# A four-layer graph network on one core: the third layer sums over the edges before its weight product

## What is computed

```python
x = x + L0(h)   # x1 = h @ W1 + b1 (512 wide), four gated sums over the edges, concatenated
x = x + L1(h)   # h @ W.T + bias, W scattered from edge_weight
x = x + L2(h)   # GCN, the layer of the change
x = x + L3(h)   # attention over the edges, elu
```

```python
deg = segment_sum(1, dst + loops); dinv = rsqrt(deg)
h = h @ W
out = segment_sum(h[src] * (dinv[src] * dinv[dst])[:, None], dst) + b
return relu(out)
```

## Time and profile before

| | us |
|---|---|
| three runs | 1003.13, 1002.95, 1000.69; median 1002.95 |
| the profiled execution | 1001.58, span 1000.0 |
| PE busy | 977.4 |
| DVE, ACT, POOL busy | 668.7, 430.9, 140.4 |

### The profile page before, as it was taken

How to read it: one execution, slowest core, us unless ns; L and a number is a source line. 1 busy time by engine, 2 the same in 40 slices (tenths; PEclk the granted TensorE clock), 3 DMA queues, 4 the chain that set the end, 5 groups by cost and what they waited for, 6 DMA issues and landing times.

```text
span 1000.0 us, 14720 instructions
## 1 busy us (share of the span) xinstructions
PE 977.4 (98%) x5170; PEld 809.6 (81%) x5170; DVE 668.7 (67%) x1221; ACT 430.9 (43%) x650; POOL 140.4 (14%) x191
## 2 busy tenths in 40 slices
PE   5999999999999999999999999999999999999997
PEld 3788788888888888888888888888888888888886
DVE  7877888788778879354485343216446664988886
ACT  5688865554543646112242322233222232445543
POOL 3022500000000010232221000000110000333331
PEclk9999999999999999999999999999999999999999
DMA  7256580000000014745433111243451230101223
GB/s 251 101 177 222 136 255 1 1 22 0 0 21 0 0 12 104 178 171 188 180 124 116 42 42 43 77 155 106 156 180 69 69 121 0 43 22 64 84 84 122
DMA packets 27326, 93.42 MB, mean 93 GB/s; under 512 B 3530, under 2 KB 3530, under 8 KB 27136
## 3 DMA queue, kind: packets, MB, share of 16 engines
q1 hardware_dynamic: 16400, 58.07, 16.5%
q0 software_dynamic: 10880, 34.74, 11.4%
HBM read 64.48 MB, written 33.56 MB: 98 GB/s over the span
## 4 chain that ended last, share of the span: by engine, by line
PE 91%; DVE 5%; ACT 2%; issue 1%; POOL 1%; DMA 0%; ACTq 0%; DVEq 0%; POOLq 0%
PE ps L592 32%; PE ps L2052 11%; PE ps L1972 9%; PE ps L1974 9%; PE ps L1973 9%; PE ps L2025 5%; PE ps L2024 5%; PE ps L575 3%; PE ps L1895 1%; PE ps L1897 1%; PE ps L1896 1%; PE ps L1866 1%; PE ps L1822 1%; PE ps L1825 1%; PE ps L1838 1%
## 5 line engine op out<-in xcount | busy, mean ns | idle before, releaser
L1972 PE MATMUL ps<-g_hi,mask_hi 128*128 128x512 f32 x400 | 157.4, 394 | 2.1 <-DVE mask_lo L1513 2.1
L1974 PE MATMUL ps<-g_hi,mask_lo 128*128 128x512 f32 x400 | 155.9, 390 | 0.0
L1973 PE MATMUL ps<-g_lo,mask_hi 128*128 128x512 f32 x400 | 155.7, 389 | 0.0
L558 ACT ACTIVATE hT_hi<-ps 128x1024 fp32r<-128x1024 f32 x40 | 41.0, 1025 | 200.3 <-PE ps L575 200.3
L592 PE MATMUL ps<-w_hi,hT_hi 128*128 128x512 f32 x320 | 126.4, 395 | 0.0
L592 PE MATMUL ps<-w_lo,hT_hi 128*128 128x512 f32 x320 | 124.7, 390 | 0.0
L2052 PE MATMUL ps<-y_all,att_hi 128*128 128x512 f32 x400 | 110.0, 393 | 1.5 <-DVE att_lo L1693 1.5
L1110 ACT ACTIVATE mask<-ps,v 128x640 f32<-128x640 f32 x80 | 63.4, 793 | 111.2 <-PE ps L1974 52.9
L592 PE MATMUL ps<-w_hi,hT_lo 128*128 128x512 f32 x320 | 98.6, 389 | 0.0
L1972 PEld LDWEIGHTS ps<-g_hi,mask_hi 128*128 128x128 f32 x400 | 75.1, 188 | 20.4 <-DVE mask_lo L1513 3.3
L2052 PEld LDWEIGHTS ps<-y_all,att_hi 128*128 128x128 f32 x400 | 74.0, 188 | 17.3 <-DVE att_lo L1693 1.5
(11 more groups left out here) (203 smaller groups left out, 1839.2 us busy)
## 6 DMA issues: line engine op xcount, KB each, us to landing
xin<-x_after SPq DMA_DIRECT2D x30, 512.0 KB, 3.3
xres<-x_after POOLq DMA_DIRECT2D x20, 512.0 KB, 4.2
x_after<-xres POOLq DMA_DIRECT2D x20, 512.0 KB, 3.0
w_raw<-in_L_gnn_W SPq DMA_DIRECT2D x8, 1024.0 KB, 7.2
x_after<-g POOLq DMA_DIRECT2D x20, 256.0 KB, 7.4
xres<-x_after SPq DMA_DIRECT2D x10, 512.0 KB, 3.4
xin<-in_x SPq DMA_DIRECT2D x9, 512.0 KB, 3.4
out_x<-xres SPq DMA_DIRECT2D x9, 512.0 KB, 2.7
```

Source lines behind the costliest of these rows:

```text
L1972: nc.tensor.matmul(SUMS[dd], mask_hi[k][:, cols], g_hi[:, s, :], start=(s == 0), stop=False)
L1973: nc.tensor.matmul(SUMS[dd], mask_hi[k][:, cols], g_lo[:, s, :], start=False, stop=False)
L1974: last = nc.tensor.matmul(SUMS[dd], mask_lo[k][:, cols], g_hi[:, s, :], start=False, stop=(s == T - 1))
```

## The change

The third layer is computed as (C h) W. Its parts:

- **Rows.** There is no reload of `x` for the third layer's norm. While the second layer's product runs, DVE takes the statistics of the finished rows in `xres` (`hs_stats_of`), ACT subtracts the mean and applies relu (`hs_relu`) and makes the high part times scale and dinv (`hs_hi_of`), DVE the low part (`hs_lo_of`). POOL's reload of `xres` waits for that relu. The loops over the second layer's tiles are written out.
- **Sums.** Six passes: two halves f of the 1024 features, by three ranges c of destination nodes of 512, 226 and 512 columns (in the order 0, 2, 1). A pass has ten steps; a step holds blocks of normed rows stationary (four blocks of features, high and low) and moves the counts of the range, converted by ACT into a ring of four. The result is already transposed for the product; it leaves PSUM as a high part (ACT) and a low part (DVE) into `sums_w` and `sums_x`, a pair of banks at a time. Passes alternate between two sets of four banks.
- **Product.** `gcn_product`, 48 matmuls of 512 columns per tile, the transposed sums stationary, W moving; then `gcn_out` as before, now per tile.
- **Weights.** W of the third layer is loaded after the third pass and split in the fifth and sixth; W of the last layer is loaded after the last pass and split beside the products, its destination taking the place of sums that are used up.
- The five semaphores `mask_used` and `cnt_used` become one each; nothing else of the first layer is changed.

```diff
+WIDTHS = (BANK, BANK, N - 2 * BANK)
+PASSES = [(f, c) for f in range(2) for c in (0, 2, 1)]
+COUNT_RING = 4
@@ DVE
+        def hs_stats_of(t):
+            b = t % 2
+            dve.wait_ge(res_added, t + 1)
+            for half in range(2):
+                hs_step_done(nc.vector.bn_stats(stats[b][:, half, :], xres[b][:, half * 512:(half + 1) * 512]))
...
+        def hs_scale_of(i):
+            dve.wait_ge(hs_root_ready, i + 1)
+            hs_step_done(nc.vector.reciprocal(rough[:, :], hs_root[:, :]))
+            dve.wait_ge(hs_chain, hs_steps[0])
+            hs_step_done(nc.vector.tensor_tensor(square[:, :], rough[:, :], rough[:, :], ALU.mult))
...
+        def hs_lo_of(t):
+            dve.wait_ge(hs_hi_ready, t + 1)
+            dve.wait_ge(hs_scale_ready, t // 2 + 1)
+            nc.vector.scalar_tensor_tensor(hs[:, :, t, 1, :], hs_f[:, :, t, 1, :], hs_scale[:, t % 2:t % 2 + 1], hs[:, :, t, 0, :].bitcast(F32),
+                                           ALU.mult, ALU.subtract).then_inc(hs_lo_ready, 1)
...
-        dense_dve(dve, d2, y_rest, late=self_loops)
+        for t in range(T):
+            if t >= 3:
+                hs_lo_of(t - 3)
+            if t + 2 < T:
+                stats_dve(dve, d1, (t + 2) // 2, t % 2)
+            if t + 1 < T:
+                transposed_dve(dve, d1, (t + 1) // 2, (t + 1) % 2)
+            if t % 2 == 1 and t + 2 < T:
+                variance_dve(dve, d1, (t + 2) // 2)
+            if t >= 1:
+                hs_stats_of(t - 1)
+            if t % 2 == 0 and t >= 2:
+                hs_variance_of(t // 2 - 1)
+            if t == 2:
+                self_loops()
+            residual(t)
+            if t % 2 == 1 and t + 2 < T:
+                scale_dve(dve, d1, (t + 2) // 2)
+            if t % 2 == 0 and t >= 2:
+                hs_scale_of(t // 2 - 1)
@@ ACT
+        for t in range(T):
+            if t % 2 == 1 and t >= 3:
+                hs_hi_of(t - 3)
+            if t + 1 < T:
+                transposed_act(act, d, (t + 1) // 2, (t + 1) % 2)
+            if t + 2 < T:
+                h_act(act, d, (t + 2) // 2, t % 2)
+            if t % 2 == 1 and t >= 3:
+                hs_hi_of(t - 2)
+            if t == T - 1:
+                for n in range(COUNT_RING):
+                    counts_act(n)
+            if t >= 1:
+                hs_relu(t - 1)
...
+        for n in range(T * len(PASSES)):
+            if n + COUNT_RING < T * len(PASSES):
+                counts_act(n + COUNT_RING)
+            if n == 0:
+                hs_relu(T - 1)
+            if n == 1:
+                hs_root_of(HT - 1)
+            if n == 2:
+                hs_hi_of(T - 2)
+            if n == 3:
+                hs_hi_of(T - 1)
+            if n == last_pass - HT:
+                split_act(act, dense[2], range(2))
+            if last_pass <= n < last_pass + KT - 2:
+                act.wait_ge(cnt_used, n + 1)
+                split_act(act, dense[2], [n - last_pass + 2])
+            if n % T >= T - 2:
+                sums_hi_of(n // T, n % T - (T - 2))
@@ PE
-        dense_pe(pe, dense[1], dense[2], lambda b: pe.wait_ge(sum_read, T * GATES - HT + 2 + b))
-        dense_pe(pe, dense[2])
+        dense_pe(pe, dense[1], lambda b: pe.wait_ge(sum_read, T * GATES - HT + 2 + b))
+        def gcn_pass(p):
+            f, c = PASSES[p]
+            sums = [PASS_BANKS[p % 2][j // 2][:, j % 2 * BANK:j % 2 * BANK + WIDTHS[c]] for j in range(4)]
+            for s in range(T):
+                n = T * p + s
+                if p == 0:
+                    pe.wait_ge(hs_lo_ready, s + 1)
+                pe.wait_ge(cnt_ready, n + 1)
+                columns = cnt[n % COUNT_RING][:, 0:WIDTHS[c]]
...
+                    for j in (2 * pair, 2 * pair + 1):
+                        nc.tensor.matmul(sums[j], hs[:, f, s, 0, j * P:(j + 1) * P], columns, start=(s == 0), stop=False)
...
+                    for j in (2 * pair, 2 * pair + 1):
+                        last = nc.tensor.matmul(sums[j], hs[:, f, s, 1, j * P:(j + 1) * P], columns, start=False, stop=(s == T - 1))
...
+        def gcn_product(t):
+            b = t % 2
+            pe.wait_ge(product_read[b], dense[2].pairs(t // 2))
+            pe.wait_ge(sums_lo_ready, 2 * PASSES.index((1, t // PASS_TILES)) + 2)
...
+                for part, rights in ((0, (W_HI[2], W_LO[2])), (1, (W_HI[2],))):
+                    for half in range(2):
+                        for right in rights:
+                            last = nc.tensor.matmul(PRODUCT[2][b][:, half * BANK:(half + 1) * BANK], sums_tile(t, part)[:, k, :],
+                                                    right[k][:, half * BANK:(half + 1) * BANK],
```

More of the change, by code:

```diff
@@ L306, in build_program, with __init__, norm_pairs @@
     class Dense:
-        def __init__(self, n):
+        def __init__(self, n, norm):
             self.n = n
+            self.norm = norm
         def pairs(self, i):
             return HT * self.n + i
+        def norm_pairs(self, i):
+            return HT * self.norm + i
         def tiles(self, t):
[L316 to L324, removed]
+            return T * self.norm + t
+    dense = [Dense(0, 0), Dense(1, 1), Dense(2, None), Dense(3, 2)]
     dst_landed = sem("dst_landed")
@@ L519, in scale_dve @@
         settled(dve, norm_chain0, done + 4)
[L520 to L526, removed]
+        nc.vector.tensor_tensor(scale[:, :], rough[:, :], step[:, :], ALU.mult).then_inc(scale_ready, 1)
     def scale_pool(pool, i):
@@ L651, in dense_act, with sums_place, sums_bank, sums_tile @@
         transposed_act(act, d, HT - 1, 1)
[L652 to L657, removed]
-        finish(HT - 1, 0)
[L659 to L664, removed]
-        finish(HT - 1, 1)
-        if nxt is not None:
-            root_act(act, nxt, 0)
+        finish(HT - 1, 0)
+        late()
+        finish(HT - 1, 1)
+    def sums_place(p, pair, part):
+        f, c = PASSES[p]
+        blocks = slice(4 * f + 2 * pair, 4 * f + 2 * pair + 2)
+        if c < 2:
+            return sums_w[:, PASS_TILES * c:PASS_TILES * (c + 1), part, blocks, :]
+        return sums_x[:, :, part, blocks, :]
+    def sums_bank(p, pair):
+        f, c = PASSES[p]
+        tiles = PASS_TILES if c < 2 else T - 2 * PASS_TILES
+        return PASS_BANKS[p % 2][pair].rearrange("p (k n) -> p k n", n=BANK)[:, :, 0:tiles * P].rearrange("p k (t n) -> p t k n", n=P)
+    def sums_tile(t, part):
+        return sums_w[:, t, part, :, :] if t < 2 * PASS_TILES else sums_x[:, t - 2 * PASS_TILES, part, :, :]
     def load_weights(eng, d, dram):
         for q in range(4):
-            eng.dma_start(W_RAW[d.n][:, 2 * q:2 * q + 2, :],
+            eng.dma_start(W_PAIRS[d.n][q],
                           dram[2 * q * P:(2 * q + 2) * P, :].rearrange("(k p) n -> p k n", p=P)
@@ L904, in _ @@
             pool.wait_ge(half_stored[i], 32)
[L905 to L912, removed]
+        load1(0)
+        load1(1)
+        for t in range(T):
+            store1(t)
+            if t + 2 < T:
+                load1(t + 2)
+        d = dense[2]
         def load2(i, b):
@@ L1175, in y_act @@
+        for k in range(KT):
+            act.wait_ge(product_ready[k % 2], dense[2].pairs(k // 2 + 1))
+            split_act(act, dense[3], [k])
+            if k == KT - 3:
+                h_act(act, dense[3], 0, 0)
+                h_act(act, dense[3], 0, 1)
+        transposed_act(act, dense[3], 0, 0)
+        root_act(act, dense[3], 0)
         def y_act(d, i, b):
@@ L1976, in half_pe @@
                         last.then_inc(sum_ready, 1)
[L1977 removed]
+                last.then_inc(mask_used, 1)
         half_pe(0, 0, 0)
@@ L2036, in spread_al @@
+        for t in range(T):
+            gcn_product(t)
         def spread_al(tiles):
```

429 lines of the change are left out of this document (232 added, 197 removed).

## The result

The changed kernel takes 993.13 us (median of four, 992.32 to 993.59), the kernel before 1002.39 (median of four beside it, 1000.69 to 1003.13): a ratio of 0.991, 95% interval 0.9898 to 0.9921. Faster by 9.3 us; the forecast was 995, 7.4 less than this median of before and 8 less than the one known then. The profiled execution took 993.59 us, its span 991.7. Ratios compare fast executions; one of the ten of the experiment that puts the transposes back took 3061 us and stands outside them, without a trace that says why.

The account below looks back on a forecast made before the run. TensorE, busy 98% of the span, was taken as the bound. 1001.6 less 8.7 (transposes) and 0.1 (sums), plus 0.7 and 0.3 (waits), gave 993.8; the median 1.4 higher gave 995, range 991 to 1008.

Parts of the forecast that it names:

- The bound and the transposes: TensorE bounds throughout; in the third layer eighty transposes go, ten tiles of eight, 8.7 us less, nothing hides them.
- rival B: In the second layer's product VectorE becomes the bound, every second tile 1 to 2 us late: 999 to 1005; chance 0.14.
- The narrow matmul: In two of six sums passes, 160 matmuls of 226 columns at 112 ns each, 17.9 us; sums 90.6 against 90.7.
- rival C: In the third layer's sums, narrow matmuls lose the one-pass pace, 397 ns each, 45.6 us in all: 1040; chance 0.16.
- rival D: In the third layer's sums, a narrow matmul lies between 112 and 227 ns: half of 18.4 us, 1004; chance 0.06.
- The second layer's product: Beside it VectorE also prepares the third layer's rows: 20.3 of 23.6 us per tile pair, hidden with 0.9 us to spare.
- Some sixteen gaps of 0.15 us: Between VectorE's dependent operations beside the second layer's product, 2.4 us per pair of tiles.
- the 0.7 us charged for the self loops: In tile 2 of the second layer's product, ten additions of 0.28 us make the next `hT_lo` about 0.7 us late.
- The seam: From the second layer's product into pass 0: last rows ready some 15 us later, count 7 about on time; 0.3 us charged.
- The sum: Whole kernel, profiled execution: 1001.6 - 8.7 - 0.1 + 0.7 + 0.3 = 993.8; the median is 1.4 higher, so 995.

## Why the prediction was right

**The bound and the transposes.** "10 x 0.87 = 8.7 us less" is what the stages show (8.73), and putting bare transposes back took the kernel to 1.000 of the one before. PE waited for nothing from the first matmul of the second layer's product to the last layer's product, so the sign of rival B, PE idle before every second product, didn't come.

**The narrow matmul.** Predicted 112 ns, measured 111.6; the sums 90.6 against 90.48. The number was taken from the rhythm of the weight loads in the earlier trace rows, and the floor that it means is there: it stands from 64 to 226 columns, and at 256 and above the stream takes over with the wide one's fixed 13.8 ns. What the floor is made of stays open, as said above. With it falls rival C: no narrow float32r matmul took two records or 397 ns, and rival D: nothing lay between. The Trainium skill (TensorE: Matmul & The Clock Gate, Back-to-back issue gap) gives N/2.4 + 2.5 ns for a matmul by itself, an estimated 97 ns here, and about 81 ns at 128 columns and 131 at 512 for a stream of weight loads and matmuls; the prediction named only the first. This case's stream took 111.6 ns at 226 and 227.1 at 512, so neither holds for these float32r matmuls. The skill's section on LDWEIGHTS gives 128 columns / 1.2, 107 ns; the floor lies 5 ns above it.

**The second layer's product.** VectorE's load was predicted well, 20.3 us of 23.6, and measured 20.45 in the stretch above. The step that failed is the count of gaps. "Some sixteen gaps of 0.15 us" and the 0.7 us charged for the self loops: the chain of the new rows has gaps of 0.03 us, not 0.15, and ten self-loop additions took 2.11 us from start to end, not 2.8. The residual behind them started 0.5 us after its product (445.51 against 445.02) where the prediction had 1.9. The tile after them shows it:

```profile
443.49 2.11 DVE L1706 TENSOR_TENSOR countT<-countT,ident 128x128 int16<-128x128 int16 x10
...
446.90 2.41 DVE L1686 TENSOR_TENSOR square<-rough 128x2 f32<-128x2 f32 x1
449.34 0.16 DVE L1688 TENSOR_TENSOR square<-square,hs_variance 128x2 f32<-128x2 f32 x1
449.54 0.17 DVE L1690 TENSOR_SCALAR step<-square 128x2 f32<-128x2 f32 x1
...
454.32 1.21 DVE L584 TENSOR_TENSOR hT_lo<-ps,hT_hi 128x1024 fp32r<-128x1024 f32 x1
```

This `hT_lo` ends at 455.53; PE wants it at 451.37 + 5.45 = 456.82, behind the second half of the tile's matmuls. It is 1.3 us early where the sum had it 0.7 late. The 2.41 us of `square` are as predicted.

**The seam.** Charged 0.3 us, cost nothing. The last remainder of the rows ends 13.7 us after the product (539.08 + 1.28 - 526.67), not 15, and is wanted at 16.4; count 7 is there 1.4 us early (538.0 against 526.67 + 12.7), not on the dot:

```profile
539.08 1.28 DVE L1700 SCALAR_TENSOR_TENSOR hs<-hs_f,hs_scale,hs 128x1024 fp32r<-128x1024 f32 x1 [0.28 <-ACT hs L1193]
```

**The sum.** 8.7 + 0.1 - 1.0 was predicted against the profiled execution, 9.28 measured in the stages. The difference of 1.5 us is the 1.0 us of waits that didn't come, and about half a microsecond of matmul pitch. The prediction priced every wide matmul at 227.1 ns, the pitch of a tile with transposes in it. Where no transposes stand between them they come every 226.7 ns in the new product, and in the sums of the kernel before every 226.8 ((91.57 - 0.87) / 400). That gives the 0.33 us in the product, which came back with the transposes, and the 0.12 in the sums beyond the predicted 0.1. The profiled execution came out 0.2 us from its 993.8, and that close by luck: its second layer's product began 1.1 us later than before, which hid most of the 1.5.

## What to carry to other kernels

Where PE is busy throughout, an order of products that leaves the result already transposed is worth the transposes' own time and little else (9.1 us of 9.3 here), if the preparation still fits beside it. Read the fit from the other queue's throughput over a whole period, start to start, and not from the slack of one operation. A matmul with a weight load of its own has a floor, here 112 ns; by the two measured terms it is reached at about 235 columns ((111.6 - 13.8) x 2.4, an estimate), and trimming columns below that bought nothing. When an operation on a handful of values takes microseconds, look at what the other engines do at that moment.

## What the runs showed of the hardware

- float32r matmuls with a load each, start to start at the full clock: 112 ns at 64 columns, 112 at 192, 111.6 at 226, 119.9 at 256, 147 at 320, 226.7 at 512, and 227.1 to 227.7 where transposes stand between them. At half the clock: 213 ns at 64 columns, 427 at 512.
- PE fell to half its clock while it issued matmuls of 64 columns without a gap (granted clock 0.50 from 549 to 557); with 192 columns it kept the full clock. So a PE that is busy all the time by the profile had lost its clock here.
- Operations of VectorE on 128 x 2 values, with two operands (TENSOR_TENSOR) and with one (TENSOR_SCALAR) alike, were held until the end of a GpSimd addition: 2.4 us when they began with it, up to 2.85 when they began during the issue of a transfer just ahead of it. In the kernel with two extra operations `step` was held for 2.83 us from 472.54, while GpSimd issued a transfer (472.37 to 472.91) and added (472.92 to 475.32). Transfers without an addition held none of them above 0.24 us. It goes the other way as well: in the changed kernel the addition that began at 528.21, during a remainder of VectorE (527.97 to 529.25), took 3.30 us instead of 2.41. Statistics were not held: in the kernel before, two of them took 1.28 us from 468.90, beside an addition that began at 469.18.
